# Folding the keys and values of a second attention inside an FFN stage instead of ahead of the attention

## The reference, cut to what matters

```python
x = x + ffn(layernorm(x), w_gate, w_up, w_down)   # with 16-bit rounding of whole tensors by their maxima
# second attention: 16 heads of 64, context (4, 77, 192) and one null key per head
q = layer_norm(x, g_norm) @ Wq
k, v = split(context @ Wkv)
k, v = concat([null_k, k]), concat([null_v, v])   # masked keys excluded
out = softmax(q @ k.T / 8) @ v                    # by heads
x = x + layer_norm(out @ Wout, g_out)
# then a mixture of 8 experts, top 2
```

## Time and profile before

| what | us |
|---|---|
| median of 3 runs (1245.01 to 1251.27) | 1246.44 |
| profiled execution | 1250.26 |
| its span, first to last instruction | 1248.5 |
| third FFN stage | 486 to 546 |
| fourth FFN stage | 546.3 to 624.5 |
| preparation of the second attention | 624.5 to 692.9 |
| PE, DVE, ACT, POOL busy in the span | 1074.1, 954.4, 620.5, 428.0 |

### The profile page before, as it was taken

The page is one execution under the profiler, slowest core; times in us unless marked ns, Lnnn a source line. Parts: engine busy times, 40 slices in busy tenths (PEclk is TensorE's granted clock), DMA queues, the critical chain, the costliest instruction groups (busy, mean ns, idle before and its releaser), DMA issues. The chain is left out here.

```text
span 1248.5 us, 21557 instructions
## 1 busy us (share of the span) xinstructions
PE 1074.1 (86%) x6208; PEld 897.2 (72%) x6208; DVE 954.4 (76%) x2586; ACT 620.5 (50%) x1332; POOL 428.0 (34%) x514
## 2 busy tenths in 40 slices
PE   7899999995998981039977599999999969999998
PEld 5677777874886760039944588888898858788786
DVE  4798998874675998976554677788878758888886
ACT  1667766761565996977445233333333322333333
POOL 1344444440001882000011235544554443334333
PEclk9999999995998995559999799999999988999999
DMA  8000000000233765702213500101000000000000
GB/s 264 1 2 2 1 1 1 2 1 29 107 120 122 265 252 197 236 22 64 68 43 106 174 1 1 42 0 42 0 0 0 1 1 9 25 18 17 25 17 26
DMA packets 35551, 71.87 MB, mean 58 GB/s; under 512 B 3531, under 2 KB 23071, under 8 KB 35295
## 3 DMA queue, kind: packets, MB, share of 16 engines
q1 hardware_dynamic: 34111, 70.28, 16.9%
q10 hardware_dynamic: 1376, 0.79, 0.3%
HBM read 40.41 MB, written 30.65 MB: 57 GB/s over the span
## 5 line engine op out<-in xcount | busy, mean ns | idle before, releaser
L1068 PE MATMUL a_ps<-VW,a_PT 128*128 (+1 forms) x640 | 143.7, 379 | 0.0
L1068 PEld LDWEIGHTS a_ps<-VW,a_PT 128*128 128x128 f32 x640 | 119.3, 190 | 15.2
L1106 ACT ACTIVATE a_U<-a_U 128x1280 f32<-128x1280 f32 x32 | 40.6, 1270 | 112.6 <-DVE a_U L1179 112.6
L1085 ACT COPY a_PT<-a_ps 128x512 f32<-128x512 f32 (+1 forms) x96 | 46.1, 518 | 90.2 <-PE a_ps L1031 90.2
L1171 DVE TENSOR_REDUCE a_mx<-a_ps 128x4 f32<-128x320 f32 x128 | 62.4, 487 | 33.2 <-PE a_ps L1017 33.0
L1920 PE MATMUL m_ps<-m_wh,m_xh 128*128 128x512 f32 x256 | 87.1, 422 | 0.0
L2018 POOL TENSOR_TENSOR m_half<-m_half 128x512 f32<-128x512 f32 x32 | 41.1, 1283 | 131.9 <-ACT m_half L1980 131.9
L854 DVE TENSOR_SCALAR a_U<-a_ps 128x320 f32<-128x320 f32 x128 | 59.3, 484 | 30.2 <-PE a_ps L662 20.9
L1920 PE MATMUL m_ps<-m_wh,m_xl 128*128 128x512 f32 x256 | 82.0, 402 | 0.0
L1920 PE MATMUL m_ps<-m_wl,m_xh 128*128 128x512 f32 x256 | 81.4, 399 | 0.0
L745 PEld LDWEIGHTS a_ps<-vals,a_PT 128*128 128x128 f32 x640 | 79.7, 199 | 2.2 <-issue 0.4
(11 more groups left out here) (250 smaller groups left out, 3159.2 us busy)
## 6 DMA issues: line engine op xcount, KB each, us to landing
up_scratch<-f_ub SPq DMA_DIRECT2D x24, 512.0 KB, 3.0
f_ul<-up_scratch SPq DMA_DIRECT2D x24, 512.0 KB, 4.5
vw_scratch<-vw_stage SPq DMA_DIRECT2D x8, 640.0 KB, 4.2
VW<-vw_scratch SPq DMA_DIRECT2D x4, 1280.0 KB, 5.8
xs<-in_x SPq DMA_DIRECT2D x4, 1024.0 KB, 12.6
h_scratch<-f_hh SPq DMA_DIRECT2D x8, 512.0 KB, 2.7
h_scratch<-f_hl SPq DMA_DIRECT2D x8, 512.0 KB, 3.2
f_bh<-h_scratch SPq DMA_DIRECT2D x8, 512.0 KB, 4.4
```

Of the source, the lines that this page charges most:

```text
L1068: last = pe.matmul(Y[:, 0:D], PTs[t.p][:, j, :], c["VW"][:].rearrange("p b j d -> p (b j d)")[:, bass.ds(t.batch % 2 * (NJ * D) + j * D, D ...
L1085: act.copy(PTs[t.p][:, js[0]:js[-1] + 1, :].rearrange("p j n -> p (j n)"), R[k][:, 0:len(js) * P]).then_inc(s_PTe, 1)
```

## The change

The block of `prepare1` is gone; a class `Prepare1` does its work inside the third FFN stage, in the order written out there for each engine. Weights are no longer loaded whole: for each head pair SP loads two pieces of `Wkv` (96 x 2 x 128 numbers each), one of `Wq` and one of `Wout` (128 KB each), each two buffers deep. Null key and null value are both added on POOL. ACT copies folded keys unsplit to a stage, and SP stores them to a new DRAM scratch (640 KB a pair); values are stored in two halves of 320 KB a pair. POOL, not ACT, rounds the up products of a unit in place (by adding a large constant `ROUND`, which DVE's product subtracts again). The small inputs (context, mask, null vectors, norm weights) are loaded at the head of the second FFN stage.

Folded keys stand in SBUF for two batches, not four. Those of batch 0 are loaded unsplit in the fourth FFN stage and split there (`high_half` on ACT, `low_half` on DVE, 1280 columns each, twice). Those of batches 1 to 3 are loaded (1.3 MB) and split in quarters of 640 columns behind tiles 0 to 3, 8 to 11 and 16 to 19 of the attention (`SPLIT`). `gout` is loaded at the attention's start, and POOL waits for it first. The attention's loops, and the fourth stage's on ACT and DVE, are written out in full.

```diff
-class Early:
...
-def prepare1(nc, st, sem, retired, sbuf, c):
...
+class FoldedKeys:
...
+    def load_raw(self, sp, b, s_kr=None):
+        for k in range(KT):
+            sp.dma_start(self.raw[:, k, :].rearrange("p (m n) -> p m n", n=2 * KP),
+                         self.kscr[:, :, k, b, :].rearrange("m p n -> p m n")).then_inc(s_kr or self.s_kr, 16)
...
+    def high_quarter(self, act, b, q):
+        cols = slice(q * QW, (q + 1) * QW)
+        return act.copy(self.high[b % 2][:, :, cols], self.raw[:, :, cols])
+    def low_quarter(self, dve, b, q):
+        cols = slice(q * QW, (q + 1) * QW)
+        return dve.tensor_tensor(self.low[b % 2][:, :, cols], self.raw[:, :, cols],
+                                 self.high[b % 2][:, :, cols].bitcast(F32), ALU.subtract)
...
+class Prepare1:
...
+    def load_keys(self, sp, m):
+        if m >= 2:
+            sp.wait_ge(self.s_A, 4 * (m - 1))
...
+    def load_out(self, sp, m):
+        if m >= 2:
+            sp.wait_ge(self.s_W, 2 * (m - 1))
...
+    def store_keys(self, sp, m):
+        sp.wait_ge(self.s_Ae, 4 * m + 4)
+        sp.dma_start(self.kscr[m].rearrange("p k b n -> p (k b n)"),
+                     self.keys[m % 2][:].rearrange("p k b n -> p (k b n)")).then_inc(self.s_ks[m % 2], 16)
+    def store_values(self, sp, m, half):
+        sp.wait_ge(self.s_We, 4 * m + 2 * half + 2)
...
+    def stored(self, eng):
+        for i in range(2):
+            eng.wait_ge(self.s_ks[i], 16 * self.NM // 2)
+            eng.wait_ge(self.s_st[i], 16 * self.NM)
...
+    def folded_key(self, pe, m, i):
+        hh, k = i % 2, i // 2
+        if i == 0:
+            pe.wait_ge(self.s_ke, m + 1)
+            pe.wait_ge(self.s_Te, 2 * m + 2)
+        if m >= 1:
+            pe.wait_ge(self.s_Ae, 4 * (m - 1) + i + 1)
+        if i >= 2 and m + 1 < self.NM:
+            self.query_T(pe, m + 1, i - 2)
+        pe.matmul(self.AB[i][:, 0:B * KP], self.wqT[m % 2][hh * D1:(hh + 1) * D1, k, :],
+                  self.k1[m % 2][hh * D1:(hh + 1) * D1, :], start=True, stop=True).then_inc(self.s_A, 1)
...
+    def key_out(self, act, m, i):
+        hh, k = i % 2, i // 2
+        act.wait_ge(self.s_A, 4 * m + i + 1)
+        if i == 0 and m == 0:
+            act.wait_ge(self.s_gs, 1)
+        if i == 0 and m >= 2:
+            act.wait_ge(self.s_ks[m % 2], 16 * (m // 2))
+        if i >= 2 and m + 1 < self.NM:
+            self.query_out(act, m + 1, i - 2)
+        act.activation(self.keys[m % 2][:, k, :, hh * KP:(hh + 1) * KP],
+                       self.AB[i][:, 0:B * KP].rearrange("p (b k) -> p b k", b=B), ACT.Copy,
+                       scale=self.gsc[:, k:k + 1]).then_inc(self.s_Ae, 1)
+    def value_out(self, act, m, half):
+        act.wait_ge(self.s_W, 2 * m + half + 1)
+        if m >= 1:
+            act.wait_ge(self.s_st[half], 16 * m)
+        for hh in range(2):
+            act.copy(self.stage[half][:, hh, :], self.WB[hh][0:KP, :]).then_inc(self.s_We, 1)
...
+    def null_key(self, pool, m):
+        if m == 0:
+            pool.wait_ge(self.s_nv, 6)
+        pool.wait_ge(self.s_km, m + 1)
+        pool.tensor_tensor(self.k1[m % 2][:], self.k1[m % 2][:], self.nm[:].rearrange("p b k -> p (b k)"),
+                           ALU.add).then_inc(self.s_ke, 1)
...
+                fold.load_gout(sp)
+                retired.clear(sp)
+                for b in range(1, B):
+                    if b >= 2:
+                        sp.wait_ge(s_kl, 4 * (b - 1))
+                    fold.load_raw(sp, b, s_kr)
                     if b >= 2:
                         sp.wait_ge(s_y, TPB * (b - 1))
-                    sp.dma_start(c["VW"][:, b % 2], c["vscr"][:, :, b * D:(b + 1) * D].rearrange("h k d -> (h k) d")
-                                 .rearrange("(j p) d -> p j d", p=P)).then_inc(s_vw, 16)
+                    fold.load_values(sp, b)
                     if b == 1:
                         mw.load(sp)
...
+                def high(b, q):
+                    if q == 0:
+                        act.wait_ge(s_kr, 32 * b)
+                        if b >= 2:
+                            act.wait_ge(s_S, 4 * TPB * (b - 1))
+                    fold.high_quarter(act, b, q).then_inc(s_kh, 1)
+                for t in range(FIRST, LAST + 1):
+                    body(At(t))
+                    if t in SPLIT:
+                        high(*SPLIT[t])
...
+                pool.wait_ge(c["s_go"], 16)
...
+            NM = p1.NM
             @block.scalar
             def _(act):
-                def ints(t):
-                    if t.t0 >= 2:
-                        act.wait_ge(s_pr, t.of(lambda n: n - 1))
-                    act.activation(gq[t.p][:], unit(t.n), ACT.Copy, scale=ksl).then_inc(s_g3, 1)
-                    act.wait_ge(s_ul[t.t0 % 4], 16 * (t.t0 // 4 + 1))
-                    act.activation(uq[t.p][:], ul[t.t0 % 4][:], ACT.Copy, scale=kup).then_inc(s_uq, 1)
-                for t in range(NU):
-                    ints(At(t))
+                def ints(u):
+                    if u >= 2:
+                        act.wait_ge(s_pr, u - 1)
+                    act.activation(gq[u % 2][:], unit(u), ACT.Copy, scale=ksl).then_inc(s_g3, 1)
+                ints(0)
+                ints(1)
+                p1.key_scale(act)
+                for k in range(KT):
+                    act.wait_ge(p1.s_T, k + 1)
+                    p1.query_out(act, 0, k)
+                for m in range(NM):
+                    p1.key_out(act, m, 0)
+                    p1.key_out(act, m, 1)
+                    if 3 * m + 2 < NU:
+                        ints(3 * m + 2)
+                    if m >= 1:
+                        p1.value_out(act, m - 1, 0)
+                    p1.key_out(act, m, 2)
+                    if 3 * m + 3 < NU:
+                        ints(3 * m + 3)
+                    p1.key_out(act, m, 3)
+                    if m >= 1:
+                        p1.value_out(act, m - 1, 1)
+                    if 3 * m + 4 < NU:
+                        ints(3 * m + 4)
+                p1.value_out(act, NM - 1, 0)
+                p1.value_out(act, NM - 1, 1)
             @block.sync
             def _(sp):
-                for t in range(4, NU):
-                    sp.wait_ge(s_uq, t - 3)
-                    load(sp, At(t))
+                p1.load_keys(sp, 0)
+                p1.load_values(sp, 0)
+                p1.load_keys(sp, 1)
+                p1.load_out(sp, 0)
+                def more(u):
+                    if u < NU:
+                        sp.wait_ge(s_pr, u - 3)
+                        load(sp, At(u))
+                for m in range(NM):
+                    more(3 * m + 4)
+                    if m + 1 < NM:
+                        p1.load_values(sp, m + 1)
+                        p1.load_out(sp, m + 1)
+                    if m >= 1:
+                        p1.store_values(sp, m - 1, 0)
+                    more(3 * m + 5)
+                    if m + 2 < NM:
+                        p1.load_keys(sp, m + 2)
+                    p1.store_keys(sp, m)
+                    more(3 * m + 6)
+                    if m >= 1:
+                        p1.store_values(sp, m - 1, 1)
+                p1.store_values(sp, NM - 1, 0)
+                p1.store_values(sp, NM - 1, 1)
             @block.tensor
             def _(pe):
+                p1.query_T(pe, 0, 0)
+                p1.query_T(pe, 0, 1)
+                p1.key_product(pe, 0)
+                for m in range(NM):
+                    p1.value_product(pe, m)
+                    if m + 1 < NM:
+                        p1.key_product(pe, m + 1)
+                    p1.folded_key(pe, m, 0)
+                    p1.folded_key(pe, m, 1)
+                    if m >= 1:
+                        p1.folded_value(pe, m - 1, 0)
+                    p1.folded_key(pe, m, 2)
+                    p1.folded_key(pe, m, 3)
+                    if m >= 1:
+                        p1.folded_value(pe, m - 1, 1)
+                p1.folded_value(pe, NM - 1, 0)
+                p1.folded_value(pe, NM - 1, 1)
+                pe.wait_ge(p1.s_We, 4 * NM)
                 rows_max(pe, 4)
                 spread_max(pe, 4)
+            @block.gpsimd
+            def _(pool):
+                def rounded(u):
+                    if u < NU:
+                        v = ul[u % 4][:]
+                        pool.wait_ge(s_ul[u % 4], 16 * (u // 4 + 1))
+                        pool.tensor_scalar(v, v, kup, ROUND, ALU.mult, ALU.add).then_inc(s_uq, 1)
+                p1.constants(pool)
+                rounded(0)
+                rounded(1)
+                p1.null_key(pool, 0)
+                for m in range(NM):
+                    rounded(3 * m + 2)
+                    p1.null_value(pool, m)
+                    rounded(3 * m + 3)
+                    if m + 1 < NM:
+                        p1.null_key(pool, m + 1)
+                    rounded(3 * m + 4)
             @block.vector
             def _(dve):
-                def body(t):
```

(98 more changed lines are left out.)

411 lines of the change are left out of this document (181 added, 230 removed).

## The result

The changed kernel takes 1242.93 us (median of 18 runs, 1234.47 to 1251.32) against 1246.54 before (18 runs, 1241.84 to 1251.27). The ratio is 0.9969, its 95% interval 0.9954 to 0.9984: a gain of 0.3%, less than the 0.5% that counts as a change here, and 40 us above the forecast of 1202.7 and above its range. The profiled execution took 1245.74 us.

The account below looks back on a forecast made before the run. TensorE bounds the attention's main loop, ACT and DVE passes the third FFN stage, no engine the preparation. -67.9 + 21.4 + 1.8 + 1.0 = -43.7 against 1246.44: 1202.7 us; own range 1196 to 1210, 80% range 1189 to 1222.

Parts of the forecast that it names:

- the paragraph on queue order: Third FFN stage, SP's queue: a unit load behind the waits for `s_W` and `s_Ae` is covered by 1.6 us.
- The last sentence of the prediction: Third FFN stage: it would be wrong above all by waits in a ring among four in-order engines; no size given.
- The sum of the engines: Third FFN stage: DVE sets 8.6 us a head pair, ACT 8.0; stage 82 us instead of 60.6, +21.4.
- Preparation removed: Before the second attention: 68.4 us that fill no engine go, less one stage border of 0.5: -67.9 us.
- `gout`: Attention start: POOL waits for this 128 KB load before its first rsqrt: +1.8 us (1.2 to 2.1).
- Key splits: Fourth FFN stage: nothing; attention: 12 each on ACT and DVE, nearly all hidden: +1.0 us (bounds 0 and 17.9).
- the term that the prediction took as 0 within 4: Loops written out: at most some 4 us won in the attention's main loop, as much lost; taken as 0.
- Rival A: Third FFN stage bound by DMA: stage 90.2 us, kernel 1211 us; 20 in 100.
- Rival D: TensorE stays at 1.2 GHz through the third FFN stage: stage 134.8 us, kernel 1255 us; 5 in 100.
- Rival E: Third FFN stage: transfers go one behind the other, 30.2 us a pair, stage 256, 1377 in all; 1 in 100.
- B: Cheaper: DVE and POOL seldom collide, third FFN stage 78.1 us, `gout` 1.2, splits free: kernel 1197 us; 12 in 100.
- C: Attention: splits lie in the path, DVE's low half waiting for ACT's high half: +16.9, kernel 1220 us; 5 in 100.

Follow-up runs that it names:

- e8: e5 with g_out loaded in the fourth FFN stage and value weights ahead of the unit load in SP's round: 1200.96 us, ratio 0.9624.
- e11: e8 with eight idle 128x128 matmuls on TensorE ahead of each value product from the third pair on: 1196.23 us, ratio 0.9596.
- e12: The changed kernel with eight idle 128x128 matmuls on TensorE ahead of each value product from the third pair on: 1243.18 us.
- e3: The changed kernel with key weights first in SP's round, their wait relaxed by one pair, and the output weights' load last: 1213.27 us, ratio 0.9735.
- e10: e5 with eight idle 128x128 matmuls on TensorE ahead of each value product from the third pair on: 1208.0 us.
- e5: e3 with the stores of folded keys and values issued by ACT behind its own copies, not by SP: 1210.52 us.

## Why the prediction was wrong, point by point

**The step that failed is the paragraph on queue order.** It took the wait for `s_W` on SP, asked only for the unit load behind it, and found it covered by 1.6 us. Two things stand behind that wait that it didn't follow: the key and query weights of a later pair, and, at the end of their flight, TensorE's key product, which has the folded values in its own queue. Those are what the wait is for. A wait that stands, over some steps, in front of what ends it is not covered by a constant; it sets a period, the sum of the steps around the circle. Here, by the timeline: 1.3 us from the output weights' issue to that of the key weights, 0.9 for the two issues, 5.4 to the start of the product, 2.4 for it at half clock, 6.1 to the end of the folded values: 16.1 in this turn, 16.8 on average. The cover of 1.6 us was also worked out from ACT's pace of 8 us a pair, which the circle does not allow: it assumed its result.

The last sentence of the prediction named this failure, but gave it no price and no chance. Much of the price could have been had from the rows: 4.4 for a landing, with the products and copies between them from the earlier trace rows.

**The sum of the engines came near for a queue without the circle.** ACT was busy 58.1 us in e8's stage, 7.3 a pair: less than the forecast 8.0, which took passes 1.13 apart where ACT's own start 1.04 apart. DVE: 34.8 + 28.9 + 3.9 + 3.8 = 71.4, 8.9 a pair (8.6); it stayed the busiest, but at 83% of the stage, not over 90%. POOL: 31.3 + 11.6 + 11.5 = 54.4, 6.8 (7.4 to 8.4; a pass took 1.31 us on average, between the 1.04 and 1.91 of the earlier trace rows, so it lost less to products than forecast, while its sums took 1.44, against 0.86 in the earlier trace rows). The first folded-key copy came at 494.40, 10.1 us after e8's stage began (12.6). From the third pair's to the eighth's, 513.43 to 556.14, e8 took 8.5 us a pair on average (7.3 to 11.0). What it has over the 82 forecast lies between the second pair and the third, 13.4 us (500.07 to 513.43), where TensorE waits 3.27 us for value weights and then runs at half clock. So a reordered queue comes near the forecast's 1202.7 (1200.96, which early `g_out` lowers by some 2.75); the nearness is part luck, since e8's stage is 3.7 us over and the stretch of the attention's tiles 3.4 under the forecast.

**Preparation removed:** -68.1 against -67.9, right, and the clock gave nothing back, as argued: in the attention's first 10 us it was 0.54 before and 0.62 after, in the next 10 us 1.00 before and 0.86 after. The fourth FFN stage took 78.5 us against 78.2, so its key splits were hidden, as forecast.

**`gout`:** the mechanism was right, its size was not: POOL waited 3.64 us and the attention's start grew by 3.2, not 1.8 (bounds 1.2 to 2.1). The bounds came from landings of whole-width loads and stores (the 2.1 of the earlier trace rows; for the 3.0 those rows have nothing), though the trace of before has this very load, in its fourth stage among large weight loads, at 11.2 us. Here the load, a row of 1 KB spread to all 128 partitions, was issued at 688.49 and let POOL go at 692.44, 3.95 us later, with the first keys' and values' loads of the attention issued right behind it.

**Key splits:** +1.0 forecast, -2.4 measured from first to last row sum. ACT's 12 pieces took 0.71 us and DVE's 0.83 on average, while DVE's waits for scores in the stretch fell from 30.9 to 20.1 us. The pace of the tiles settles both. In the changed kernel most row sums start 9.53 us apart, in tiles with splits as in those without (the 23rd to the 28th); where splits begin an interval grows by 0.95, where they end one shrinks by as much. Before, in the hardware loop, they started in turn 9.41 and 9.85 us apart, 9.63 on average. So the 0.1 us a tile, some 2.7 us over 27 tiles, came with the loops written out, the term that the prediction took as 0 within 4, and the splits cost some 0.4 us net, in the first tiles (the second interval is 8.44 us and not 7.07, one behind the first four splits 0.94 shorter). No run changed the one without the other.

**Rival A (DMA bound, 90.2 for the stage):** refuted in two ways. e8's and e11's stages are shorter than 90.2 with the same 24.66 MB, and 5.24 MB more cost 2.9 to 3.6 us. The whole traffic took 83% of the 16 engines over 85.7 us, 71 us, between the two prices of 67 and 82 that the prediction had. (Its stages for them, 75.5 and 90.2, differ by 14.7 and not by 15.2; nothing hangs on it.) Single loads land later in this traffic (below), and in e8 four of the six 10 us windows from 496 us on have a DMA share of 1.01 to 1.04: there the engines of the DMA are full, and no run doubled the stores on e8, so what bounds e8 itself is not shown.

**Rival D (half clock throughout):** its stage of 134.8 us comes nearest to the 126.1 measured, but by luck. The clock was 0.68 on average, not 0.50, and the products at half clock were those behind the waits for key weights, so the half clock came with the waits and lengthened the circle that made them, by some 3 us a turn (the estimate under e12). It does not explain the stage alone: e3 kept a mean clock of 0.75 and lost 29 us of the stage. Where the circle was cut, the half clock costs some 3 us of stage (e10, one trace).

**Rival E (transfers one behind another):** the runs don't bear it out. The weight loads of 96 and 128 KB flew beside unit loads and stores, and a 10 us window of e8 moved 388 GB/s. What the runs show of those small loads is the cost of their place in the queue. The Trainium skill's advice to batch transfers to 1 MiB and more (DMA: Bandwidth & Descriptors, section Bandwidth) is not tested: no run here varied a load's size.

**B and C:** C is refuted by the tiles' pace. Of B, the free splits came true and POOL's fewer collisions, but not its `gout` of 1.2 us; beside 40 us both are small.

TensorE's wait for the third pair's value weights is there in e3, e5, e8 and e10 (2.8 to 3.3 us). In e8's trace their buffer was free at 492.6, when the first value product ended; the load went out at 499.90, behind three unit loads and three weight loads, and the product began at 507.42. So 7.3 us went by in SP's queue and 7.5 more from issue to use; no run moved this load further ahead.

What stays open: what the half clock costs in the circle (no run had the circle at full clock), and the share of the landing time in it that is owed to other traffic.

## What to carry to other kernels

When a stage adds loads to an in-order DMA queue, write down for every wait in that queue all that is behind it until the next wait, who uses each of those, and what that user has queued behind it; if that path comes back to what the first wait is for, its period is the sum of its steps, landing time included, and where that is longer it replaces the sum of the busiest engine. What helped here left ACT's and DVE's work as it was: loads whose wait is long met go first, a wait for the newest result goes last, and stores go on the queue of the engine that makes what they store (126 us to 86, in four moves). The sign here was a stage in which neither an engine nor the DMA engines were more than two thirds busy.

## What the runs showed of the hardware that was not expected

Loads land later in mixed traffic: by medians, a unit of 512 KB took 6.6 us in the changed kernel's third stage and 6.0 in e5's, against 4.4 in the stage before the change, though the changed kernel's DMA engines were only 60% busy. Its weight loads of 96 to 128 KB took 4.5 us (keys), 5.2 (queries) and 6.3 (values), the last nearly as long as a unit, which is over five times as large; the output weights, 128 KB too, which go out first after a lull, took 2.1, and in e5, where they don't, 5.4.

The granted clock changed between its two levels many times within one stage: by 10 us windows from 496 us on, e8 had 1.00, 0.50, 0.99, 1.00, 0.83, 1.00. It fell in a window in which TensorE was busy 8.6 of 10 us (506 to 516), after a wait of 3.3 us for value weights, and came back in the next. From 538 to 540 us it was 0.50 again, after a wait of 2.1 us. The same four-instruction product took 1.24 us at one level (e8's L550) and 2.47 at the other (L547 of the changed kernel). With the eight idle matmuls put where the wait is, the stage was 3.2 us shorter in e10 and 1.8 in e11; put ahead of another wait, as in e12, they left the next product at 2.47.
